# A hybrid layer stack on one core: half of the output product goes into the chain over states, half of V between the two triangles, the gate's products together

## What is computed

```python
q = silu(x @ Wq.T).reshape(b, n, h, hd)          # 16 heads of 32
k = silu(x @ Wk.T).reshape(b, n, h, hd)
v = (x @ Wv.T).reshape(b, n, h, hd)
beta = 2.0 * jax.nn.sigmoid(x @ Wbeta.T)
k = k * jax.lax.rsqrt(jnp.sum(k * k, axis=-1, keepdims=True) + EPS)
# for each token: S += k (beta (v - k S));  o = q S
o = _delta_rule(q, k, v, beta).reshape(b, n, d)
gate = jax.nn.sigmoid(x @ Wg1.T @ Wg2.T)
og = (o * gate).reshape(b, n, h, hd)
rms = jax.lax.rsqrt(jnp.mean(og * og, axis=-1, keepdims=True) + EPS)
return (og * rms).reshape(b, n, d) * g_norm @ Wo.T
```

## Time and profile before

| | us |
|---|---|
| median of 3 runs | 5107.09 (5098.03 to 5112.65) |
| the profiled execution | 5093.37, of which its span is 5091.6 |
| PE busy in the span | 4591.6 (90%) |
| DVE, ACT, POOL busy | 3620.3 (71%), 2409.6 (47%), 716.3 (14%) |
| mean granted TensorE clock | 0.965 |

### The profile page before, as it was taken

The page is one execution under the profiler, slowest core; times in us unless marked ns, Lnnn a source line. Parts: engine busy times, 40 slices in busy tenths (PEclk is TensorE's granted clock), DMA queues, the critical chain, the costliest instruction groups (busy, mean ns, idle before and its releaser), DMA issues.

```text
span 5091.6 us, 144724 instructions
## 1 busy us (share of the span) xinstructions
PE 4591.6 (90%) x63104; PEld 3229.5 (63%) x63104; DVE 3620.3 (71%) x7890; ACT 2409.6 (47%) x4592; POOL 716.3 (14%) x909
## 2 busy tenths in 40 slices
PE   5799999999999998499999999999999999999998
PEld 4677777777777776346546645655654664665564
DVE  3667766666767666387787678678778767867866
ACT  3234333333333343164564565466456456546645
POOL 0000000000000000112211211221221121122121
PEclk9899999999999998699999999999999999999999
DMA  2222222222222222100000000000000000000000
GB/s 61 48 66 69 65 65 67 61 62 61 62 61 65 64 68 61 64 1 18 1 18 18 18 1 18 18 2 18 18 2 18 18 13 6 18 18 1 18 9 10
DMA packets 352134, 171.76 MB, mean 34 GB/s; under 512 B 300016, under 2 KB 300784, under 8 KB 350736
## 3 DMA queue, kind: packets, MB, share of 16 engines
q1 hardware_dynamic: 342528, 145.20, 10.7%
q10 hardware_dynamic: 8976, 17.30, 1.2%
HBM read 93.74 MB, written 67.63 MB: 32 GB/s over the span
## 4 chain that ended last, share of the span: by engine, by line
PE 43%; DVE 10%; ACT 3%; issue 1%; POOL 1%; DMA 1%; SPq 0%; DVEq 0%; ACTq 0%; POOLq 0%
PE row_psum L1687 9%; PE row_psum L1661 9%; PE row_psum L40 5%; DVE smax L1938 5%; PE row_psum L42 5%; PE row_psum L41 5%; PE row_psum L1675 4%; PE row_psum L1729 1%; ACT xr_hi L1310 1%; PE row_psum L1713 1%; DVE probs L1918 1%; PE row_psum L1451 1%; DVE stats L1772 1%; POOL rstd L1253 1%; PE row_psum L1633 1%
## 5 line engine op out<-in xcount | busy, mean ns | idle before, releaser
L1938 DVE TENSOR_REDUCE smax<-row_psum 128x1 f32<-128x512 f32 x2048 | 1269.3, 681 | 90.9 <-PE row_psum L1661 90.4
L1386 ACT ACTIVATE probs<-row_psum 128x512 f32<-128x512 f32 x2048 | 1096.6, 602 | 378.1 <-PE row_psum L1675 358.5
L1661 PE MATMUL row_psum<-k_stack,q_stack 64*128 64x512 f32 (+1 forms) x2048 | 738.3, 437 | 50.6 <-DVE smax L1938 24.4
L1675 PE MATMUL row_psum<-q_stack,k_stack 64*128 64x512 f32 (+1 forms) x2048 | 761.6, 447 | 17.4 <-DMA q_stack<-shift 4.4
L1661 PEld LDWEIGHTS row_psum<-k_stack,q_stack 64*128 64x128 f32 (+1 forms) x2048 | 350.5, 186 | 504.1 <-DVE smax L1938 374.0
L1687 PE MATMUL row_psum<-probs,v_aug 128*32 128x512 f32 x4096 | 539.5, 604 | 2.3 <-ACT av_sb L1402 0.8
L1675 PEld LDWEIGHTS row_psum<-q_stack,k_stack 64*128 64x128 f32 (+1 forms) x2048 | 340.9, 185 | 211.7 <-ACT probs L1386 152.3
L868 DVE TENSOR_TENSOR lane_t<-lane_t,lane_p 128x30 f32<-128x30 f32 (+14 forms) x960 | 318.3, 332 | 33.0
L40 PE MATMUL span_bank<-x_hi,w_hi 128*128 128x256 f32 x1024 | 303.1, 296 | 32.5 <-DVE x_lo L841 32.5
L865 DVE TENSOR_TENSOR lane_p<-lane_t 128x30 f32<-128x30 f32 (+14 forms) x960 | 315.6, 329 | 23.5
L40 PE MATMUL row_psum<-wf_hi,xr_hi 128*128 128x320 f32 (+1 forms) x1024 | 327.1, 319 | 0.5 <-DVE xr_lo L1806 0.3
(11 more groups left out here) (209 smaller groups left out, 9867.4 us busy)
## 6 DMA issues: line engine op xcount, KB each, us to landing
x_sp<-in_x ACTq DMA_DIRECT2D x33, 512.0 KB, 4.0
tri_dram<-tri SPq DMA_DIRECT2D x256, 64.0 KB, 2.0
lane_t<-tri_dram SPq DMA_DIRECT2D x32, 512.0 KB, 4.7
inv_dram<-lane_t SPq DMA_DIRECT2D x32, 512.0 KB, 2.6
inv_b<-inv_dram SPq DMA_DIRECT2D x256, 64.0 KB, 2.3
x_res<-in_x SPq DMA_DIRECT2D x32, 512.0 KB, 3.9
x<-x_res SPq DMA_DIRECT2D x32, 512.0 KB, 3.7
xs<-x SPq DMA_DIRECT2D x16, 1024.0 KB, 5.6
```

The lines of the kernel that those rows point to most:

```text
L1386: act.activation(probs[:, h % PROBS, tt, :], ps[:, m % STACK_BANKS, :], ACT.Exp, scale=float(DH) ** -0.5).then_inc(exp_ready, 1)
L1661: pe.matmul(ps[:, bank, :], q_stack[rows, qt, P * st:P * st + P], k_stack[rows, kv, :], start=True, stop=True).then_inc(max_mm, 1)
L1675: pe.matmul(ps[:, m % STACK_BANKS, :], k_stack[rows, kv, P * tt:P * tt + P], q_stack[rows, qt, :], start=True, stop=True).then_inc(score_m ...
L1938: dve.tensor_reduce(smax[:, g, st:st + 1], ps[:, bank_of("max", NT * g + st), :], AX.X, ALU.max).then_inc(max_ready, 1)
```

## The change

Four things are moved, and nothing is added or taken away.

- On PE half 1 of the output product of `behind` moves from behind `without_state` to behind `chain(0)`. The sums of the squared keys move from behind `chain(0)` to behind `chain(1)`, and the first half of the gate's products from behind `chain(1)` to behind `chain(2)`, where the second half stands.
- On PE half 1 of V moves from behind both triangles to between them.
- On DVE the residual's second addition moves from ahead of three columns of the inversion (`"inputs"`) to behind the first advance of the state and one more column.

```diff
--- before.py
+++ after.py
@@ -762,17 +762,16 @@
                 if further:
                     project_q(*further, 1)
                 without_state(*now)
+                state_inputs(*now)
+                chain(*now, 0)
                 if behind:
                     output(*behind, 1, further, ahead)
-                state_inputs(*now)
-                chain(*now, 0)
+                chain(*now, 1)
                 if further:
                     key_sums(*further, 0, behind)
-                chain(*now, 1)
+                chain(*now, 2)
                 if further:
                     project_gate(*further, 0)
-                chain(*now, 2)
-                if further:
                     project_gate(*further, 1, behind)
                 chain(*now, 3)
                 if further:
@@ -783,8 +782,8 @@
                     key_rows(*further)
                     pe.wait_ge(ln2_ready, at(*now, 2, 2))
                     triangles(*further, 0)
+                    project_v(*further, 1)
                     triangles(*further, 1)
-                    project_v(*further, 1)
 
             def end(now):
                 output(*now, 0, None, None)
@@ -973,11 +972,11 @@
                 if behind:
                     add_residual(*behind, 0)
                 invert_ahead("transitions")
-                if behind:
-                    add_residual(*behind, 1)
                 invert_ahead("inputs")
                 advance(*now, 0)
                 invert_ahead("chain0")
+                if behind:
+                    add_residual(*behind, 1)
                 advance(*now, 1)
                 invert_ahead("chain1")
                 advance(*now, 2)
```

## The result

| | before | changed |
|---|---|---|
| median, the two in one session, 4 runs each | 5102.56 (5094.89 to 5112.65) | 5289.75 (5282.89 to 5291.18) |
| span of the profiled execution | 5091.6 | 5281.1 |
| mean granted TensorE clock | 0.965 | 0.942 |

The ratio is 1.0377, with a 95% interval of 1.0353 to 1.0401. (The two medians by themselves give 1.0367, inside that interval.) The changed kernel is 3.8% slower: between the medians +187 us where +109 was forecast, and above the top of the range, 5265.

A forecast was written before the change was run, and what follows sets the result against it. In the attention part PE's work in its own order plus its idle time was taken to bound the kernel. V's move +50, instruction supply +49 and clock +10 gave +109 on 5107.1, so 5216 us, range 5155 to 5265.

The forecast's parts named there:

- the low clock behind the turn: First product for k, behind the turn's new idle time: loses 1.5 us in 6 steps of 10, +26 us, bounds 0 to +44.
- part 1: V's half 1 between the triangles: later turn and low clock behind it, +50 us, from +24 to +68.
- part 2: Output product inside the chain: +49 us for instruction supply and +10 for the clock.
- net of wait, `x_lo` and V: Around the turn: later turn, less `x_lo` idle time and V's low clock won back, +24 us.
- fetch term: L664, L674 and first chain step: one run of 320 records stalls for instructions, +1.7 us a step, +49, bounds 0 to +87.
- clock term: Output product at the low clock, +42, later falls about 13, less the chain's earlier 45: +10 us, bounds -20 to +40.
- edits at nothing: DVE's addition, sums, gate halves, SP's store and load, POOL's subtraction: later or moved at no cost, 0 us.
- both, with the clock low behind both new idle times in every step: Rival: low clock behind the turn's and L674's idle time in every step, +158 us, 5265 us; chance 0.10.
- Only part 1: Rival: only V's move costs; the run's stall merely replaces the chain's, 5157 us; chance 0.13.
- only part 2: Rival: only the output product's move costs; DVE masks sooner or V's clock repays all, 5166 us; chance 0.08.
- Faster: Rival: the 320-record run costs nothing; the chain's stalls and low clock go, 5048 us; chance 0.04.

The follow-up runs named there:

- v_fill: Kernel before with only V's half 1 between the triangles, plus twelve unread large matmuls behind the triangles; 1.0080 of the kernel before.
- v_fill6: Kernel before with only V's half 1 between the triangles, plus six unread large matmuls behind the triangles; 1.0082 of the kernel before.
- o_only: Kernel before with only the output product moved into the chain, gate's products together and DVE's addition moved; V in its old place; 1.0110, +56 us.
- o_fill: `o_only` plus output product half 0 once more, unread, between L664 and L674; 1.0064 of the kernel before.
- g_only: Kernel before with only the gate's two halves together between the third and fourth chain step; 0.9998 of the kernel before.
- o_nog: `o_only` with the gate's halves apart, the first behind the second chain step; 1.0123 of the kernel before.
- v_fill3: Kernel before with only V's half 1 between the triangles, plus three unread large matmuls behind the triangles; 1.0287 of the kernel before.
- v_early: Kernel before with V's half 1 between the triangles and DVE's normalisation moved ahead of the masks; 0.9975 of the kernel before.
- v_best: `v_early` with the first column of DVE's inversion moved behind the first two corrections of the lower halves; 0.9907 of the kernel before.

## Why the prediction was wrong in size

**The step that failed** is the low clock behind the turn: "I take 6 steps in 10: 29 x 0.6 x 1.5 = +26; bounds 0 and +44". Three things in it were too small.

- How often. It was 29 steps of 29. The start-up had shown it 2 times of 2, with the same neighbours, triangles ahead and small tiles behind. I discounted that without a row that spoke for less.
- What stands in it. I charged the first product for k alone. The turn (1.97 - 1.09 = 0.9 us) and L561 (3.62 - 1.98 = 1.6 us) run at the low clock ahead of it, and the turn's 1.97 us stood in the earlier trace rows already. With the product for k it is 105 / 28 = 3.75 us a step.
- The bounds. +44 came from the same 1.5 us in all steps, so the range could not reach the time. With 29 x 3.75 = +109 in place of +26 the sum is 5216 + 83 = 5299, 9 us above the measured time. That it comes so near is in part luck, since smaller errors cancel: by the table above the rest of part 1 is 7 us above its forecast, part 2 is 18 below its +59, and 13 us lie outside the 28 steps.

`v_fill` and `v_fill6` show that this term is the clock and not the wait: both keep the turn as late and give the clock back, and the time falls by 105 and some 100 us.

**Right in part 1.** The idle time of 2.7 us ahead of the turn was 2.9, with L834 as the one waited for in every step. The wait for `x_lo` went. V's passes no longer run at the low clock: -20 us at work from L701 to the turn, just the 14 x 1.4 us that I had put against the wait. The net of wait, `x_lo` and V is 79 - 28 - 20 = +31 where I had +24. In the forecast the turn came 2.5 us later in all 29 steps (72.5 - 29 - 19.6 = +24), and it was 79 us in 28. The other 5 us, the longer wait of L539, I had nowhere.

**Part 2 held in its time and in the stalls.** Forecast +59 (49 + 10), measured +56 alone (`o_only`) and +41 in the table of the changed kernel. The fetch term was +49 and is +43. Where the stalls fell was right too: L674 in every step, a second stall in half of the steps, and little in the chain behind the first step; `o_fill` shows that the length of the run makes them. The clock term of +10 has the work from L664 to L701 against it, -7 in the changed kernel and +3 in `o_only`, within its bounds, but its three terms were off one by one. The output product took more than the 3.1 us of full clock in 21 of 28 steps (I had 9 of 10), and it lost 0.9 us on average where I had 1.4: +24 us instead of +42. What the chain lost before I had put at 45; the low clock lasted 68.9 us there in the 28 steps, which costs 35 at most. What still falls later I had put at 13. Beside the product it fell on L674, L685 and L691 (27 us at the low clock) and no longer on the sums and the gate's products (44 us before, 0 after), which by the rows above took 30 us less in 29 steps. And of the 95.6 us at the low clock after the change 17 lie in idle time, where they cost nothing. On the supply of instructions the Trainium skill ("Runtime: NRT & Kernel Launch", "Instruction fetch mechanics") says that refills are mostly hidden. The traces bear that out at most where large products fill the packet; in the run of small tiles PE stood idle ahead of L674 in every step, 2.0 us on average and 2.7 at most.

**The edits at nothing** cost little. The gate's products cost nothing (`g_only` is 0.9998), and no new wait for `x_res` or the residual shows on PE. But L539 waits 5 us longer for the keys in all, 17.3 us in `o_only` and `o_nog` and 10.1 in `g_only`, so it comes with the output product, the sums or DVE's addition; which of them it is no run parts.

**The rivals.** The one nearest to the truth was "both, with the clock low behind both new idle times in every step", with a chance of 0.10 and +158 us. Its mechanism came for the turn in every step and for the output product in 21 of 28. It was priced from the same 1.5 us, so it too fell short. "Only part 1" and "only part 2" are out, since the two parts measured alone add up. "Faster" needed L674 without a stall, and L674 has 29.

## What to carry to other kernels

When a wait is put into a place where small tiles stand on both sides, price it as the wait plus everything at the low clock until the engine is back at full speed; look for the same neighbours elsewhere in the trace, and unless a row speaks against it take how often the clock fell there as it stands. Here a wait of 2.9 us cost another 3.75 us of slow work behind it. Before moving work on the busy engine to cover a wait, look whether the engine waited for can do the awaited work earlier: the normalisation needed nothing from the triangles, and moving it was worth more than any order on PE that was tried.

## What the runs showed of the hardware that I had not expected

- More work made the kernel faster, three times: against the same kernel without it, 12 matmuls of 512 columns a step in the idle time ahead of the turn took 105 us off (`v_fill`), 6 of them some 100 us (`v_fill6`), and 12 in the run of small tiles some 23 us (`o_fill`).
- In the same place 1.4 us of idle time left the clock at its upper level in all 29 steps (`v_fill6`), and 2.1 us brought it down in 28 of 29 (`v_fill3`). What lies between was not tried, nor whether it is the idle time or the added matmuls ahead of it that decide.
- DVE's normalisation of two tiles took 1.94 to 1.97 us where POOL's `o_lo` ran beside it (before, and after: 949.88 against POOL's 950.05) and 1.00 us where POOL did nothing (`v_early`). Of the two instructions of a step one took 1.50 to 1.53 us before and the other 0.53 to 0.55; in `v_early` and `v_best` every one took 0.53 to 0.55. No run changed POOL's work alone, so that it is POOL is argued from these rows, not shown.
